# Dealing the queries, heads and projection matmuls of images 1 to 3 between the 512-column matmuls of an expert's first layer

## The reference

```
x = x + conv(layernorm over channels of x)
  # conv: the image is cut into 7 x 7 cells of 8 x 8 pixels; sf = mean of each cell
  # aff = softmax(pixel . 9 neighbouring cell means)
  # sft = aff-weighted sums of pixels, normalised        (49 super tokens x 96)
  # qkv = qkv_w @ sft;  attention with 8 heads of 12 channels over the 49 super tokens
  # out = proj_w @ attention + proj_b;  pix_out = out of the 9 neighbours, weighted by aff
t = tokens of x
t = t + sum over the 2 best of 4 experts:  gate * (gelu(layernorm(t) @ w1[e] + b1[e]) @ w2[e] + b2[e])
```

## Time and profile before

| | |
|---|---|
| median of 3 runs | 479.98 us (479.69 to 481.36) |
| the profiled execution | 484.26 us |
| its span, first to last instruction | 482.4 us |
| PE busy, share of the span | 98% |
| DVE, ACT, POOL busy | 85%, 70%, 32% |
| weight loads (PEld) | 72% |
| mean granted TensorE clock | 0.943 |

### The profile page before, as it was taken

How to read it: one execution, slowest core, us unless ns; L and a number is a source line. 1 busy time by engine, 2 the same in 40 slices (tenths; PEclk the granted TensorE clock), 3 DMA queues, 4 the chain that set the end, 5 groups by cost and what they waited for, 6 DMA issues and landing times.

```text
span 482.4 us, 13934 instructions
## 1 busy us (share of the span) xinstructions
PE 472.0 (98%) x5695; PEld 344.9 (72%) x5695; DVE 408.7 (85%) x1102; ACT 337.5 (70%) x321; POOL 154.4 (32%) x289
## 2 busy tenths in 40 slices
PE   9999999999999999999999999999999999999997
PEld 5898785777777787676677887677666666666666
DVE  7557697877989998988899988988899888899886
ACT  1026215668797867868877769778977977999983
POOL 4134020384044186313253382113271651111100
PEclk9658556999999999999999999999999999999999
DMA  8836013315220022625020022126110221042100
GB/s 241 299 120 183 9 35 71 75 40 94 58 60 18 1 52 54 134 47 115 15 54 18 5 51 52 34 50 120 34 26 18 52 51 36 24 77 52 26 18 22
DMA packets 65324, 30.63 MB, mean 63 GB/s; under 512 B 63230, under 2 KB 63366, under 8 KB 64869
## 3 DMA queue, kind: packets, MB, share of 16 engines
q1 hardware_dynamic: 64146, 27.45, 25.1%
q10 hardware_dynamic: 1114, 2.29, 1.4%
HBM read 12.33 MB, written 4.82 MB: 36 GB/s over the span
## 4 chain that ended last, share of the span: by engine, by line
PE 75%; DVE 12%; ACT 4%; DMA 3%; issue 3%; POOL 3%; SPq 0%; DVEq 0%; POOLq 0%; ACTq 0%
PE ps L1431 22%; PE ps L1461 17%; PE ps L1466 8%; PE ps L1276 6%; PE ps L1437 5%; PE ps L1289 5%; PE ps L1453 4%; DVE hl L1095 3%; DMA xt<-xtok 3%; DVE xt L1111 3%; PE ps L1369 2%; ACT h L764 2%; PE ps L1256 1%; DVE xs L1015 1%; PE ps L1414 1%
## 5 line engine op out<-in xcount | busy, mean ns | idle before, releaser
L764 ACT ACTIVATE h<-ps 128x1536 f32<-128x1536 f32 (+1 forms) x100 | 142.5, 1425 | 55.6 <-PE ps L1437 52.3
L1095 DVE TENSOR_TENSOR hl<-h,hh 128x1536 f16<-128x1536 f32 (+1 forms) x91 | 161.0, 1774 | 7.0 <-issue 6.7
L772 ACT CAST hh<-h 128x1536 f16<-128x1536 f32 (+1 forms) x91 | 133.3, 1465 | 2.9
L1111 DVE SCALAR_TENSOR_TENSOR xt<-ps,gl,xt 128x96 f32<-128x96 f32 (+1 forms) x400 | 99.8, 309 | 25.3 <-PE ps L1466 18.9
L534 POOL TENSOR_TENSOR x<-xs,x 128x384 f16<-128x384 f32 (+1 forms) x28 | 37.7, 1345 | 236.7 <-ACT x L728 236.7
L1461 PE MATMUL ps<-w_hi,hh 128*128 128x96 f16 x1092 | 104.5, 207 | 0.0
L1461 PE MATMUL ps<-w_lo,hh 128*128 128x96 f16 x1092 | 103.8, 206 | 0.0
L1461 PEld LDWEIGHTS ps<-w_hi,hh 128*128 128x128 f16 x1092 | 92.7, 98 | 11.0 <-issue 7.2
L1461 PEld LDWEIGHTS ps<-w_lo,hh 128*128 128x128 f16 x1092 | 94.1, 98 | 0.0
L1431 PE MATMUL ps<-xhl,w_b 128*128 128x512 f16 (+1 forms) x336 | 87.3, 357 | 0.0
L1431 PE MATMUL ps<-xhl,w_a 128*128 128x512 f16 (+1 forms) x336 | 87.0, 358 | 0.0
(11 more groups left out here) (168 smaller groups left out, 554.2 us busy)
## 6 DMA issues: line engine op xcount, KB each, us to landing
xch<-x SPq DMA_DIRECT2D x4, 1176.0 KB, 7.7
out<-xt SPq DMA_DIRECT2D x24, 192.0 KB, 2.4
xt<-xtok SPq DMA_DIRECT2D x4, 663.0 KB, 13.0
xt<-xtok SPq DMA_DIRECT2D x4, 612.0 KB, 11.2
h<-w ACTq DMA_DIRECT2D x2, 570.0 KB
h<-w ACTq DMA_DIRECT2D x1, 576.0 KB
xhl<-x SPq DMA_TRANSPOSE x28, 3.7
wqkv_sb<-wqkv ACTq DMA_DIRECT2D x1, 228.0 KB
```

What stands on the lines that cost most here:

```text
L764: act.activation(h32[:, i % 3, :, 0:width(i)], z, ACT.Gelu, scale=1.0 / WS).then_inc(S["h_ready"], 1)
L772: act.copy(hh[:, i % 3, :, 0:width(i)], h32[:, i % 3, :, 0:width(i)]).then_inc(S["hh_ready"], 1)
L1095: dve.tensor_tensor(hl[:, i % 2, :, 0:n], h32[:, i % 3, :, 0:n], hh[:, i % 3, :, 0:n], ALU.subtract).then_inc(S["hl_ready"], 1)
L1111: ins = dve.scalar_tensor_tensor(out=xt[0:n, b, t, 0:C], in0=ps[0:n, sum_bank(i), j * C:(j + 1) * C], scalar=gl[0:n, b % 2, t, e:e + 1], i ...
```

## The change

`QKV`, `HEA` and `PRO` are added to the kinds that are dealt out. In slots 6, 9 and 10 of images 0 to 2 their half-0 matmuls no longer stand ahead of the first layer, but behind its full matmuls. `QKV` has 5 matmuls for 6 places (none behind the first full matmul, then one behind each), `HEA` has 8 (1, 1, 2, 1, 1, 2), `PRO` 0 has 5 (none, then one each). `PRO` 1 stands in half 1 and stays where it is, as one part. The waits move behind the first full matmul. The order on all other engines is the same.

```diff
-        BETWEEN_PRODUCTS = ("SF", "LOG")
+        BETWEEN_PRODUCTS = ("SF", "LOG", "QKV", "HEA", "PRO")
...
-            def queries(b):
-                pe.wait_ge(S["side_act"], reads_up_to((b, "SUPT", 0)))
-                o = bank((b, "QKV", 0))
-                for n in range(2 * GROUPS):
-                    pe.matmul(o[:, n * N:(n + 1) * N], wqkv_sb[:, n * 128:(n + 1) * 128], sfn[:], start=True,
-                              stop=True)
-                pe.matmul(o[0:N, 2 * GROUPS * N:2 * GROUPS * N + C], sfn[:], wqkv_sb[:, 2 * HEADS * ZONE:],
-                          start=True, stop=True).then_inc(S["side_done"], 1)
+            def queries(b, part, parts):
+                o = place((b, "QKV", 0))
+                if part == 0:
+                    pe.wait_ge(S["side_act"], reads_up_to((b, "SUPT", 0)))
+                    bank((b, "QKV", 0))
+                for n in share(2 * GROUPS + 1, part, parts):
+                    if n < 2 * GROUPS:
+                        pe.matmul(o[:, n * N:(n + 1) * N], wqkv_sb[:, n * 128:(n + 1) * 128], sfn[:], start=True,
+                                  stop=True)
+                    else:
+                        pe.matmul(o[0:N, 2 * GROUPS * N:2 * GROUPS * N + C], sfn[:], wqkv_sb[:, 2 * HEADS * ZONE:],
+                                  start=True, stop=True).then_inc(S["side_done"], 1)
...
-            def heads(b):
-                pe.wait_ge(S["side_act"], reads_up_to((b, "PRT", 0)))
-                o = bank((b, "HEA", 0))
-                for h in range(HEADS):
+            def heads(b, part, parts):
+                o = place((b, "HEA", 0))
+                if part == 0:
+                    pe.wait_ge(S["side_act"], reads_up_to((b, "PRT", 0)))
+                    bank((b, "HEA", 0))
+                for h in share(HEADS, part, parts):
...
-                ins.then_inc(S["side_done"], 1)
+                if part == parts - 1:
+                    ins.then_inc(S["side_done"], 1)
...
-            def project(b, k):
-                if k == 0:
-                    pe.wait_ge(S["side_act"], reads_up_to((b, "HET", 0)))
-                o = bank((b, "PRO", k))
-                for n, r in enumerate(project_rows(k)):
+            def project(b, k, part, parts):
+                o = place((b, "PRO", k))
+                if part == 0:
+                    if k == 0:
+                        pe.wait_ge(S["side_act"], reads_up_to((b, "HET", 0)))
+                    bank((b, "PRO", k))
+                for n in share(len(project_rows(k)), part, parts):
+                    r = project_rows(k)[n]
...
-                ins.then_inc(S["side_done"], 1)
+                if part == parts - 1:
+                    ins.then_inc(S["side_done"], 1)
```

More of the change, by code:

```diff
@@ L1387, in side @@
                 elif kind == "QKV":
-                    queries(b)
+                    queries(b, part, parts)
                 elif kind == "SCO":
@@ L1393, in side @@
                 elif kind == "HEA":
-                    heads(b)
+                    heads(b, part, parts)
                 elif kind == "HET":
@@ L1397, in side @@
                 elif kind == "PRO":
-                    project(b, k)
+                    project(b, k, part, parts)
                 elif kind == "PIX":
```

## The result

The changed kernel is slower. Its four runs have a median of 490.58 us (488.24 to 494.16), the kernel before 480.67 us in four runs; the ratio on record is 1.0184, 95% interval 1.0129 to 1.0238, or 6.2 to 11.4 us (the quotient of the two medians, 1.0206, lies in it). It was run again beside the experiments: 493.56 us in six runs, ratio 1.0219 (1.0163 to 1.0274). The forecast was 488.4 us, +8.4 us.

A forecast was written before the change was run, and what follows sets the result against it. PE, busy for 98% of the span, was taken to bound the kernel. Terms of 0.42 + 0.60 + 1.79 = 2.81 us an image, three images, gave +8.4 us: 488.4 us from 479.98, range 483.0 to 491.0.

The forecast's parts named there:

- rival D: All slots: the waits arise, but slack elsewhere swallows them, PE's later waits on DVE shrink; about 481 us, chance 0.08.
- QKV, +0.42 us predicted: Slot 6: layer ends 0.36 us earlier, but scores wait for DVE's read and start at 113.59 instead of 113.17.
- HEA, +0.60 us predicted: Slot 9: layer takes 3.09 us against 2.32; DVE's L965 starts at 125.75 instead of 125.15, HET follows.
- PRO, +1.79 us predicted: Slot 10: last projection result late, ACT's cast, DVE's subtraction and PRO 1 follow; PE idle about 1.2 us.
- The toll: Wherever weights change from 128 columns to 64 or fewer, or back: 0.10 us in, 0.11 us out, paid by each group.
- Rivals A and B: Shape changes cost nothing, the waits alone remain: 483.7 us, chance 0.20; or 0.05 us a switch: 485.2 us, chance 0.12.
- Rival C: Faster: the reads don't hold PE, so its shorter runs count, 1.02 us an image; 476.9 us, chance 0.05.
- Rival E: Idle time and thinner layers cost PE its clock; a slot at half speed per image adds 10 us: 498, chance 0.05.

The follow-up runs named there:

- the two wide kernels: Against the kernel before, only projection dealt out, 128 weight columns instead of 32: ratio 1.0108; only heads dealt out, 128 rows and columns instead of 49: 0.9982.
- the heads alone: Of the three kinds only HEA (slot 9) is dealt out, QKV and PRO left as in the kernel before; ratio 1.0064 to that kernel.
- the projection alone: Of the three kinds only PRO (slot 10) is dealt out, QKV and HEA left as in the kernel before; ratio 1.0184 to that kernel.
- the wide heads: Only HEA dealt out, each dealt matmul with 128 rows and 128 columns of weights instead of 49 and 49; ratio 0.9982 to the kernel before.

## Why the prediction was right

The mechanism was as predicted in all three slots, and each term was a little too small: 2.81 us an image forecast, 3.11 us measured. That the time fell in the stated range of 483.0 to 491.0 us took some luck: 490.58 us lies 0.4 us inside its end, and the repeat's 493.56 us outside. What the trace shows of the change in the slots is 9.35 us; beyond it the sum had no term for the clock, neither for its fall within the slots (1.6 us in the repeat) nor for the scatter of the start.

- **Bound.** PE's starts in the slots are the kernel's time. +9.35 us from slot 6 to the end against 3 x 3.11 us measured within the slots: no slot behind wins anything back, so rival D is out.
- **QKV, +0.42 us predicted, +0.52 measured.** The price of 0.155 us was met, and DVE started its read 2.43 us behind the slot's beginning, against 2.42 in the forecast. The missing 0.1 us lies between DVE's last copy (ends at 110.73) and the scores' first matmul (110.88): 0.15 us, where I had taken the 0.05 us of PRO 1.
- **HEA, +0.60 us predicted, +0.76 alone.** The groups cost 0.51 us instead of 0.48: the full matmul starts 0.19 us behind the first of two passes, not 0.17. The sum had taken the block's 0.83 us over sixteen passes, 0.052 us, as the step of a pass; that mean has the toll of the way out in it. In the same way QKV's 0.124 us a pass holds the change of shape to L1315. The steps alone are in the last section. Without a toll the sum had HEA at nothing; with 128 x 128 weights it was 0.17 us.
- **PRO, +1.79 us predicted, +1.86 measured.** A group costs 0.61 to 0.62 us (0.60), and the cast, the subtraction and PRO 1 follow as in the sum. PE's idle time ahead of PRO 1 is 1.03 us, not the 1.2 us forecast.
- **The toll.** Rivals A and B (no toll, half a toll) are out by the two wide kernels: without a change of shape a group falls by 0.2 us with the projection and 0.16 us with the heads, though more weights are loaded. The Trainium skill's rule in TensorEngine Tiling (Array Packing) (Tiling Modes, Key Properties), that changing the mode drains the engine, agrees with the trace in that each change costs time. The drain of 0.053 us a switch, estimated from the Trainium skill's page TensorE: Matmul & The Clock Gate, is half of what was measured: 0.11 us in and 0.09 us out with the projection.
- **Rival C** (the reads hold nobody) is out by the scores' wait of 0.81 us. With the wait covered, 0.18 us in all is left of the 1.1 us that the layer of slot 6 is shorter in the three images.
- **Rival E** (the clock falls) did not come in the first profiled execution of the change, which has full clock from slot 6 on. In the repeat it came once, in one image of three, and cost 1.6 us instead of 10: see below.

What the prediction named only in passing (L1095 and the hidden values that move with the reads) is that a late read of the projection holds PE twice, directly and through DVE's list. It made little difference to the sum: 1.86 us an image with PE's own wait in place, 5.37 / 3 = 1.79 us with it covered. But it is why putting PRO 1 later doesn't mend the change.

## What to carry to other kernels

Small matmuls between large ones are cheap only if they use the array in the same shape. In these traces weights of 96 to 103 rows and 128 columns paid no toll between 128 x 128 ones; weights of 64, 49 or 32 columns did, and so did those of 32 rows (0.31 us ahead of L1437 where the step is 0.22). There, pad the weights, or leave them in one block. And before a producer is spread over a long stretch, ask who reads its last result and what those engines have behind the read: spreading moves the last result to the end of the stretch, and takes away just the cover that the stretch gave to the reads.

## What the runs showed of the hardware that was not expected

**The clock fell inside slots that had it in full.** In the runs with the heads alone, with the projection alone and in the repeat of the change, each profile has one short stretch at half (windows of PE: stretch, its length, PE busy, granted clock; first the heads alone, slot 9 of image 1, then the projection alone, slot 10 of image 2):

```profile
228.00:230.00 2.00, 1.66 (x23) 0.82 0.00 0
230.00:232.00 2.00, 2.00 (x27) 0.50 0.00 0
232.00:234.00 2.00, 2.00 (x16) 0.82 0.00 0
234.00:236.00 2.00, 2.00 (x24) 1.00 0.01 4
```

```profile
342.00:344.00 2.00, 1.21 (x9) 1.00 0.00 0
344.00:346.00 2.00, 1.75 (x21) 0.68 0.00 0
346.00:348.00 2.00, 2.00 (x25) 0.50 0.00 0
```

Before both, PE had worked at groups with changes of shape and had then waited for DVE: 0.34 us at HET in the first, 1.03 us at PRO 1 in the second (busy 1.66 and 1.21 of 2 us). In the repeat the clock fell as in the first, behind HET of image 1. The granted clock of 0.50 is 1.2 GHz of 2.4 GHz. The stretches cost 1.3 and 1.5 us in these two and 1.6 us in the repeat (379.57 - 377.96). The kernel before shows none in its slots, though in slot 9 PEld waits 0.30 us for DVE's L1111 and then 0.36 us for L966, as long as in the change (0.61 us); the first profile of the change shows none either, with the same waits. This is the part of the loss that comes and goes with the run. Its cause stays open: no run here parts the waits from the changes of shape, and there are one or two profiles of each kernel.

**A change of shape costs about 0.2 us there and back.** From full to full it was 0.20 us less with padded weights for the projection and 0.16 us less for the heads, whose padded passes are themselves longer.

**The step of an fp32 matmul's passes, in a row and in full clock,** was 0.112 us with 128 columns of weights and 49 moving ones, 0.086 us with 32 and 100, 0.046 us with 49 and 13 (starts of the single records behind the earlier trace rows). With 128 columns of weights and only 13 moving ones, in the wide heads, it was 0.112 us again. In these forms the columns of the weights set the step, but for 32 and 100, where 32 columns of weights alone would be shorter; there the moving ones seem to set it.

**The scatter of whole runs goes with the clock ahead of the slots.** Of the runs of the kernel before, those with a mean granted clock of 0.961 took 479.2 to 480.5 us, those with 0.943 took 484.1 to 484.7 us; between them the order isn't strict (0.947: 483.6 to 485.7 us). In the profiles, slot 6 of image 0 starts at 105.4 to 106.1 us where the mean is 0.960 or 0.961, and at 110.2 to 111.3 us where it is 0.943 or 0.944. A comparison of 0.3% needs either many runs or the distances within the trace.
